# A routed expert layer on one core: the first expert layer with its weights stationary and up to 512 tokens moving

## What is computed

```python
x = x + tanh(g_xattn[0]) * xattn(layernorm(x), ctx, ctx)      # sigmoid scores, no softmax
t = rmsnorm(layernorm(x)) * norm_w
logits = t @ gate_w.T + gate_b
vals, idx = top_k(logits, 4)
G[token, idx] = softmax(vals)
h = einsum('mh,eoh->emo', t, w1) + b1                         # 512 -> 2 x 512, every expert
a = minimum(h[..., ::2], 7.0)
b = clip(h[..., 1::2], -7.0, 7.0)
act = a * sigmoid(1.702 * a) * (b + 1.0)
y = einsum('emi,edi->emd', act, w2) + b2                      # 512 -> 512
x = x + tanh(g_ffn[0]) * (layernorm(x) + einsum('me,emd->md', G, y))
```

## Time and profile before

| | |
|---|---|
| median of 3 runs | 921.92 us (921.55 to 922.35) |
| the profiled execution, own time | 924.91 us |
| its span, first to last instruction | 923.1 us |
| TensorE busy | 849.5 us, 92% of the span |
| VectorE, ACT, GpSimd busy | 573.2, 332.2, 437.4 us |
| mean granted clock of TensorE | 0.963 |
| moved by DMA | 125.38 MB, mean 136 GB/s |

### The profile page before, as it was taken

One profiled execution on the slowest core, in us unless ns is written; L12 is line 12 of the kernel. 1 busy time (PEld: TensorE's weight loads), 2 busy tenths in 40 slices (PEclk: granted clock), 3 DMA queues, 4 the chain that ended last, 5 costly groups with the idle time before them and its releaser, 6 DMA issues.

```text
span 923.1 us, 17348 instructions
## 1 busy us (share of the span) xinstructions
PE 849.5 (92%) x3770; PEld 644.9 (70%) x3771; DVE 573.2 (62%) x1023; ACT 332.2 (36%) x514; POOL 437.4 (47%) x437
## 2 busy tenths in 40 slices
PE   6889888339999999999999999999999999999993
PEld 2444444327878778788888788888878888888882
DVE  2566554607667576657667668585755758575551
ACT  3344442122525334233525534242523333332221
POOL 0255454662546455436546636363634646463331
PEclk9999999559999999999999999999999999999997
DMA  7565534162466474637466557373553737333332
GB/s 264 174 214 168 175 110 141 48 210 57 94 188 200 84 227 121 163 48 225 112 179 216 159 129 226 58 224 60 133 152 57 219 65 228 56 57 51 63 50 30
DMA packets 48431, 125.38 MB, mean 136 GB/s; under 512 B 9760, under 2 KB 9888, under 8 KB 48416
## 3 DMA queue, kind: packets, MB, share of 16 engines
q1 hardware_dynamic: 29488, 85.56, 25.9%
q0 software_dynamic: 18928, 39.66, 23.6%
HBM read 96.56 MB, written 28.94 MB: 136 GB/s over the span
## 4 chain that ended last, share of the span: by engine, by line
PE 73%; issue 9%; DMA 6%; POOL 3%; DVE 3%; ACT 3%; POOLq 0%; another core or an unknown queue 0%; DVEq 0%; ACTq 0%; SPq 0%
PE ps L431 40%; PE ps L445 20%; DMA xg<-rows,srcI 5%; PE ps L353 4%; PE ps L423 4%; PE ps L437 3%; PE ps L364 3%; POOL tab L958 2%; ACT tt L515 1%; DMA out<-ys,dgI 1%; POOL rs L949 0%; POOL out L988 0%; POOL Wl L1051 0%; ACT Qt L504 0%; DVE x L675 0%
## 5 line engine op out<-in xcount | busy, mean ns | idle before, releaser
L431 PE MATMUL ps<-Wh,xTh 128*128 x600 | 244.2, 407 | 4.1 <-ACT Wh L538 2.1
L431 PE MATMUL ps<-Wl,xTh 128*128 x600 | 238.7, 398 | 0.0
L431 PE MATMUL ps<-Wh,xTl 128*128 x600 | 237.7, 396 | 0.0
L988 POOL DMA_INDIRECT out<-ys,dgI x75 | 123.9, 1652 | 183.5 <-issue 174.5
L431 PEld LDWEIGHTS ps<-Wh,xTh 128*128 128x128 f32 x600 | 113.6, 189 | 28.4 <-issue 4.7
L431 PEld LDWEIGHTS ps<-Wl,xTh 128*128 128x128 f32 x600 | 113.4, 189 | 26.8
L985 POOL DMA_INDIRECT xg<-rows,srcI x76 | 76.9, 1012 | 114.1 <-PE ps L423 83.2
L431 PEld LDWEIGHTS ps<-Wh,xTl 128*128 128x128 f32 x600 | 113.8, 190 | 23.9
L445 PE MATMUL ps<-Wh,hTh 128*128 x300 | 125.2, 417 | 2.8 <-DVE hTl L868 2.8
L1051 POOL TENSOR_TENSOR Wl<-Wf,Wh x42 | 115.0, 2739 | 19.1 <-POOL srcI L979 10.3
L595 ACT ACTIVATE ys<-ps,dgI 128x512 f32<-128x512 f32 x75 | 51.7, 689 | 197.0 <-DVE ps L872 194.6
(11 more groups left out here) (111 smaller groups left out, 1114.1 us busy)
## 6 DMA issues: line engine op xcount, KB each, us to landing
Wf<-in_wts SPq DMA_DIRECT2D x96, 512.0 KB
Bs<-in_bias SPq DMA_DIRECT2D x16, 768.0 KB
X<-in_x SPq DMA_DIRECT2D x8, 512.0 KB, 5.9
Kt<-in_ctx SPq DMA_DIRECT2D x8, 512.0 KB, 3.8
Vt<-in_ctxT SPq DMA_DIRECT2D x8, 512.0 KB
rows<-tt SPq DMA_DIRECT2D x8, 512.0 KB, 2.8
out<-base SPq DMA_DIRECT2D x8, 512.0 KB
xg<-rows,srcI POOLq DMA_INDIRECT x76
```

The costliest lines, as they stand in the source:

```text
L431: m = e.matmul(P_[:], (xTh, xTl)[xl][:, k, :], (Wh, Wl)[wl][:, bass.ds(slot, 1), at:at + H], start=(n == 0), stop=(n == 11))
L988: e.indirect_dma_start(out, bass.IndirectOffsetOnAxis(dgI[:, i, 0:1].bitcast(I32), axis=0), ys[i][:], None, compute_op=ALU.add).then_inc(d ...
```

## The change

The loop now runs over units instead of tiles. A unit is up to four tiles of one expert. An expert of up to four tiles is one unit; one of five or six is two, the first of three tiles; one of seven or eight (none here) would be four and the rest. Each unit has a width, `F_HL`, in halves of a tile: three tiles filled to 310 tokens have width 5.

- First layer: the weights are stationary (128 x 128 blocks of `W1h`, `W1l`), and the unit's tokens move, 64 x width columns at a time. A unit has four parts (i = 0 to 3, 128 hidden channels each), a part two groups of 12 matmuls (the a half into PA, the b half into PB; two banks each). There is code for each of the eight widths in each part, chosen by nested branches (`pick`). The result has hidden channels on partitions, so `turn_h` is gone and biases are one value per partition.
- VectorE and ACT work on 256, 384 or 512 columns, by the unit's number of tiles (`pairs`).
- After part i, TensorE turns tile i of the next unit (`turn_x`). All still go through one bank, PX.
- Second layer: as before for each tile, for the unit before this one, after the four parts; PY has two banks.
- Weights: `W1h`, `W1l` and `W1f` have one place each. In an expert's last unit, ACT overwrites `W1h` part i when TensorE has read it, VectorE then `W1l` part i, and SP then loads part i of the expert after next's W1 into `W1f`. W2 has two places; its high and low pieces are made at the end of the expert's first unit. GpSimd makes no low pieces in the loop; its share goes to VectorE.
- GpSimd gathers four tiles ahead (`xg0` to `xg3`), and in one loop over j issues gather j for the unit after next and scatter j for the unit before, and waits for each scatter to land.

The core of the diff:

```diff
-            def first_layer(P_, slot, half):
-                n = 0
-                for k in range(4):
-                    at = CW * k + H * half
-                    for xl, wl in PASSES:
-                        m = e.matmul(P_[:], (xTh, xTl)[xl][:, k, :], (Wh, Wl)[wl][:, bass.ds(slot, 1), at:at + H], start=(n == 0), stop=(n == 11))
-                        n += 1
-                return m
...
+                    def part(w):
+                        if i == 0:
+                            e.wait_ge(e_xl, ready)
+                        e.wait_ge(e_lo1, made)
+                        e.wait_ge(e_af, read)
+                        e.wait_ge(e_bf, read)
+                        for h, P_, q in ((0, PA, e_l1a), (1, PB, e_l1b)):
+                            t = 0
+                            for k in range(4):
+                                for xl, wl in PASSES:
+                                    m = e.matmul(P_[i % 2][:, 0:64 * w], (W1h, W1l)[wl][:, i, 2 * k + h, :],
+                                                 (xTh, xTl)[xl][:, bass.ds(par, 1), k, 0:64 * w], start=(t == 0), stop=(t == 11))
+                                    t += 1
+                            m.then_inc(q, 1)
...
+                    pick(1, 8)
+                    with e.If(more > i):
+                        e.reg_add(turned, turned, 1)
+                        e.reg_add(landed[i], landed[i], 16)
...
+                        e.wait_ge(d_g[i], come)
+                        turn_x(i, free)
...
+                second_layer(e.snap((u + 1) % 2), e.snap(u * 4 + 4))
```

VectorE's part of a unit (`low_h`, `low_w` are the split of the hidden values and of W1):

```diff
+                    for i in range(4):
+                        now_ = e.snap(u * 4 + (i + 1))
+                        e.wait_ge(e_l1a, now_)
+                        e.tensor_scalar(av_[i % 2][:, 0:w], PA[i % 2][:, 0:w], bcur[:, 0, i:i + 1], LIMIT, op0=ALU.add, op1=ALU.min).then_inc(e_af, 1)
+                        if i:
+                            low_h(i - 1)
+                            low_w(i - 1)
+                        e.wait_ge(e_l1b, now_)
+                        e.tensor_scalar(bv[i % 2][:, 0:w], PB[i % 2][:, 0:w], bcur[:, 1, i:i + 1], 1 - LIMIT, op0=ALU.add, op1=ALU.max).then_inc(e_bf, 1)
...
+                        e.scalar_tensor_tensor(uu[:, 0:w], bv[i % 2][:, 0:w], 1 + LIMIT, av_[i % 2][:, 0:w], ALU.min, ALU.mult).then_inc(e_uu, 1)
...
+                        e.tensor_tensor(hv[i % 2][:, 0:w], uu[:, 0:w], sg[i % 2][:, 0:w], ALU.mult).then_inc(e_h, 1)
+                        with e.If(more > i):
+                            e.reg_add(split, split, 1)
+                            low_x(i, e.snap(split, min_val=5, max_val=NTILES + 8), bass.ds(odd, 1))
+                    low_h(3)
+                    low_w(3)
```

GpSimd's:

```diff
-            def landed_before():
-                e.reg_add(added, added, 16)
-                e.wait_ge(d_s, e.snap(added, min_val=16, max_val=16 * NT))
...
+            def add_back(j):
+                e.reg_add(added, added, 1)
+                e.wait_ge(e_ys, e.snap(e.snap(added, min_val=1, max_val=NTILES) + 2))
                 e.sem_inc(e_go, 1)
...
+                e.indirect_dma_start(out, bass.IndirectOffsetOnAxis(dgI[:, j, 0:1].bitcast(I32), axis=0), ys[j][:], None, compute_op=ALU.add).then_inc(d_s, 16)
+                e.wait_ge(d_s, e.snap(e.snap(added, min_val=1, max_val=NTILES) * 16))
                 e.sem_inc(e_go, 1)
...
+            with e.Fori(0, n) as u:
+                take(e.snap(u + 1))
+                e.reg_add(turned, turned, nxt[0])
+                e.wait_ge(e_tx, e.snap(turned, min_val=4, max_val=NTILES + 4))
...
+                more, back = count(fut), count(was)
+                for j in range(4):
+                    with e.If(more > j):
+                        gather(j)
+                    with e.If(back > j):
+                        add_back(j)
```

More of the change, by code:

```diff
@@ L120, in build @@
[L120 to L126, removed]
-        tt = [sb(f"tt{i}", [128, 2, H]) for i in range(2)]
-        sb = area(HI + 2 * 4 * WS, HI + 3 * 4 * WS)
+        Ri = sb("Ri", [128, E], I32)
@@ new lines, in pe @@
+            for j in range(4):
+                e.wait_ge(d_g[j], 16)
+                turn_x(j, j + 1)
+            e.wait_ge(v_te, 3)
+            n = units(e)
+            was, now, nxt = many_regs(e, "pe_was", 5), many_regs(e, "pe_now", 5), many_regs(e, "pe_nxt", 5)
+            landed = many_regs(e, "pe_landed", 4)
+            turned, done, split = e.alloc_register("pe_turned"), e.alloc_register("pe_done"), e.alloc_register("pe_split")
+            for r in landed:
+                e.reg_mov(r, 16)
@@ L611, in act @@
-            now, nxt = fields(e, "act_now"), fields(e, "act_nxt")
-            load_fields(e, nxt, 1)
-            with e.Fori(1, n) as u:
+                e.copy(xTh[:, par, :, 128 * j:128 * j + 128], px).then_inc(e_xh, 1)
+            for j in range(4):
+                high_x(j, j + 1, 0)
+            e.wait_ge(d_base, 16 * B)
+            e.wait_ge(v_te, 3)
+            n = units(e)
+            was, now, nxt = many_regs(e, "act_was", 4), many_regs(e, "act_now", 4), many_regs(e, "act_nxt", 4)
@@ L888, in dve @@
-            low_x(2)
-            product(1)
-            hidden(1)
-            for c in ON_DVE:
-                low(1, c)
-            plus_one(1)
-            with e.Fori(1, n) as u:
-                e.reg_mov(old, now[F_SLOT])
+                e.tensor_tensor(xTl[:, par, :, 128 * j:128 * j + 128], px, xTh[:, par, :, 128 * j:128 * j + 128].bitcast(F32), ALU.subtract).then_inc(e_xl, 1)
+            for j in range(4):
+                low_x(j, j + 1, 0)
+            e.wait_ge(v_te, 3)
+            n = units(e)
@@ L1022, in pool, with take @@
+            e.wait_ge(e_tx, 4)
+            place(row(nxt), 2)
+            more = count(nxt)
+            for j in range(4):
+                with e.If(more > j):
+                    gather(j)
             e.wait_ge(d_zero, 16)
             e.wait_ge(d_base, 16 * B)
-            def take(par, col):
-                e.tensor_copy(dgI[:, bass.ds(par, 1), :].rearrange("p o c -> p (o c)"), idx[:, bass.ds(col, 1), :].rearrange("p o c -> p (o c)")).then_inc(e_dg, 1)
-            def add_back(par, r):
-                e.wait_ge(e_ys, r)
+            def take(r):
+                e.tensor_copy(dgI[:], idx[:, bass.ds(row(was), 4), :]).then_inc(e_dg, 1)
+                e.wait_ge(e_dg, r)
@@ L1093, in build @@
+            take(e.snap(n + 1))
+            back = count(was)
+            for j in range(4):
+                with e.If(back > j):
+                    add_back(j)
         block = es.enter_context(nc.Block())
```

802 lines of the change are left out of this document (402 added, 400 removed).

## The result

The changed kernel takes 1354.74 us (median of 4 runs, 1351.24 to 1365.81) against 922.06 us (921.55 to 922.35): a ratio of 1.4713, 95% interval 1.4641 to 1.4785. The direction was as forecast, the size was not: 989 was predicted, with a range up to 1,095. The profiled execution took 1365.81 us over a span of 1364.0. First the page: the engines' busy time, TensorE's granted clock in 40 slices, and two DMA queues (the answer to the earlier trace rows).

The account below looks back on a forecast made before the run. TensorE, busy 92% of the span, was taken to bound the kernel. Its work falls by 50 us, but new waits bring the terms to +67.5 on 923.1: a span of 990.6, forecast 989 us, range 930 to 1,095.

Parts of the forecast that it names:

- rival 1: TensorE's longer program must be fetched at jumps, so it stands still: +80, some 1,070 us; chance 0.25.
- (g): Control: compare-and-branches around TensorE's parts, 0.25 us for half of the 96 parts: +12 us.
- (a): First layer: more but narrower matmuls on TensorE, part of each one's time fixed: -16.5 us (to -25).
- Rival 3: Narrow fp32r matmuls fall to full fp32 pace, 0.33 us at width 3: 1,050 us; chance 0.05.
- (b): TensorE's transposes of the hidden layer go, since it comes out transposed: -33 us.
- (c): Start: the first unit needs four tiles, three more passing through the one PX bank: +6 us.
- (d): VectorE's W2 pieces delay the second layer's biases, so the third tile waits for its PSUM bank: +28 us.
- (e): GpSimd's gathers stand behind the landing of scatters, so TensorE waits for tokens in narrower units: +57 us.
- Rival 2: Scatters land in under some 4 us, so waits nearly vanish: 894 us; chance 0.12.
- (h): Clock: slow TensorE matmuls after some six waits near 3 us, 1.6 us each: +10 us.
- (j): Tail: five scatters hang on the last 5 tiles, lengthening the end behind the last matmul: +10 us.

Follow-up runs that it names:

- e5: The changed kernel with code for only the five widths that occur (3, 5, 6, 7, 8) in place of eight: 1020.8 us.
- e15: e12 with code for all eight widths in place of five, same matmuls executed: 1270.4 us, one run.
- e12: e11 with a third PSUM bank (the logits') for the second layer: 892.2 us beside 921.6 for the kernel before, ratio 0.9681.
- e4: The kernel before with 2,160 never-run instructions jumped over in TensorE's loop: 931.6 us beside 924.6, one run.
- e8: e5 with GpSimd issuing all gathers of a unit before its first scatter: 977.8 us.
- e9: e8 with the W2 pieces made after the biases (VectorE) and gates (ScalarE): 954.2 us.
- e11: e9 with W1 loads issued one expert earlier and one wait for the landing of a unit's scatters together: 938.3 us.
- e13: e12 with 2,118 unused instructions jumped over in TensorE's loop and 103 unused matmuls ahead of it: 1235.6 us, one run.
- e14: e13 with 66 unused matmuls ahead of the loop in place of 103, so it lies 74 instructions earlier: 1323.6 us, one run.

## Why the prediction was wrong

**The failed step is the price of rival 1, *Code*, and with it its chance and term (g).** The right mechanism was named, down to the two rows that would show it (issue ahead of a part's first matmul, over 0.2 MB on the instruction queues). It was priced at 1 us for 120 jumps with a third hidden, +80; it is +334 (the changed kernel against e5) to +378 (e15 against e12). Three things in that step:

- It counted jumps. What is paid for is blocks: some 260 fetches of 16 KB, each round all of them, 1.3 us each (333.9 / 256), clock included. A jump over 2,160 instructions cost at most 0.1 us a round (e4).
- It took a fetch at 1 us though the nearest row of a small transfer had 3.6, and charged no slow clock to it. Idle times of 5 us came with the lower clock behind them, and TensorE's busy time grew by 109 us.
- The chance of 0.25 rested on "what runs in the loop now is brought once". That row said only that a loop of one width stays. TensorE's program, eight times as long, was on the table and should have weighed more than a rule of branches did.

**The other terms**, with code taken out: e5's span is 1021.2, the sum said 990.6, 30.6 less.

- (a) -16.5: at the full clock the spacings in e12 are 0.229, 0.203, 0.174, 0.158 and 0.114 us at 8, 7, 6, 5 and 3 halves (5.49, 4.87, 4.17 and 3.78 us for 24; 23 steps in 2.63 us at width 3). Down to 6 halves the rest beyond the columns shrinks with the width, 0.016 to 0.014; at 5 and 3 it is larger, 0.024 and 0.034. Neither bound holds throughout: the same sum gives 398 us, -21. The sum left the second layer alone, but its matmuls start 0.228 us apart in e12 (36 in 8.20 us) against 0.233 before, -4 for the 900 of them; the reason stays open. Rival 3 (0.33 at width 3) is out.
- (b) -33: the transposes are gone. (c) +6: the first part starts at 203.56 in e5 and 205.92 in e12 against 201.00, +2.6 and +4.9.
- (d) +28: its rows add up to 8.5, not 8.8, which is small beside what was missing. The wait for ys was 39.4 in e5 and 54.1 in e8. The W2 pieces are one half of the latter, 28.8 (e9); the other half, which the sum did not have, is that two banks are too few for three tiles even without the pieces, 29.0 us in e11, gone in e12.
- (e) +57: the chain was right, its size was 42.8 us, and e8 took 43.0 away. That e5's row also reads 57.0 is chance: it holds the first unit's 14.2, which the kernel before had as 16.6. Scatters took 4.7 to 4.9 us to land on the quiet tail of e8, and GpSimd waited up to 9.5 us for one in e5. Rival 2 is out, since GpSimd's 185.9 us of waits for landings stand in e5. (Its 894 also left out the 12 of (g).)
- (g) +12: TensorE's issue waits in the loop are 13.6 us in e5 and 6.5 in e12. The Trainium skill's 108 ns for a compare-and-branch (Advanced Engine Details and Errata, Control Flow Timing) would have made them an estimated 47; the trace does not show that much.
- (h) +10: the mis-sized one. TensorE's busy time falls from 834.7 in e5 to 794.0 in e12 with the same matmuls: 41. The term counted six waits near 3 us at 1.6 us each; but e11's wait of 1.86 us is already followed by eight slow matmuls, and e5 has 35 waits for tokens and ys in its loop. These 31 us are as large as the gap between 990.6 and e5, because the other misses happen to cancel: (d) +11, (j) +5 and some 7 in small ones against (e) -14, (a) -5, the second layer -4 and (c) -3.
- (j) +10: 26.8 us from the last matmul to the end in e5 against 12.2, +14.6.

e12's account closes to about 1 us: -21 (a), -4 (second layer), -33 (b), +4.9 (start), +1.7 (tail 13.9 against 12.2), and waits in the loop of 26.0 against 7.4, +18.6: -32.8, against 891.0 - 923.1 = -32.1 measured. The slow matmuls behind the waits that are left are not in it. The largest of those waits is for the split tokens (xTl, 12.9 us in the loop), since all transposes still share one bank.

## What to carry to other kernels

Count the code that one round of a loop executes, on the engine that bounds it, before specializing it by a run-time value: one variant too many, even one that is never executed, turned 1,021 us into 1,256, and the instruction queue's packets show it at once (11 against 219). A wait of TensorE costs its length and then some matmuls at half the clock (eight behind a wait of 1.86 us in e11), so price a chain of small waits at more than its sum. And look for the second wait behind the first: here code covered the gathers, these the W2 pieces, and these the missing bank.

## What the hardware showed that I had not expected

- TensorE's code stays from round to round up to a point and is then fetched whole in every round: 11 packets at a loop of 1,558 instructions, 219 at 1,802, while loops of 3,191 with an unused stretch stay (12 and 13 packets).
- The same loop 74 places further on took 88 us less (e13, e14, one run each), so that an unrelated edit ahead of a loop may move its time.
- Taking 27.3 us of waits for one bank away gave 46.1 us (e12).
